# A running sum per block in a ring of buffers, and copies of it by ScalarE, in the message stage of a graph attention kernel

## The reference, cut to what matters

```python
# N = 2500 nodes, 80000 edges, F = 512 = 8 heads x 64
h_e = einsum('nf,hfd->hnd', layernorm(x), W_e)
alpha = leaky_relu(score of each edge and head)
ex = exp(alpha - m[src])
denom = segment_sum(ex, src)                      # per node and head
msg = ex[:, :, None] * h_e[dst]                   # per edge: a row of 512
out = segment_sum(msg, src) / (denom + EPS)       # per node
```

## Time and profile before

| | us |
|---|---|
| median of 3 runs | 3220.21 (3216.58 to 3222.29) |
| the profiled execution, its own time | 3229.66 |
| its span, from first to last instruction | 3227.9 |
| the message stage in it | about 1059, from 1833 to 2892 |

### The profile page before, as it was taken

One profiled execution on the slowest core, in us unless ns is written; L12 is line 12 of the kernel. 1 busy time (PEld: TensorE's weight loads), 2 busy tenths in 40 slices (PEclk: granted clock), 3 DMA queues, 4 the chain that ended last, 5 costly groups with the idle time before them and its releaser, 6 DMA issues. The chain is left out here.

```text
span 3227.9 us, 51758 instructions
## 1 busy us (share of the span) xinstructions
PE 2604.2 (81%) x16298; PEld 1661.5 (51%) x16298; DVE 2295.9 (71%) x4733; ACT 697.2 (22%) x1316; POOL 1545.2 (48%) x1568
## 2 busy tenths in 40 slices
PE   2499987799999999999990377878787777777898
PEld 2265653577777767776760244444444444446443
DVE  3577833699999989999999667667677676775222
ACT  1133320233333333333330100000000000004321
POOL 0223311466666666555650256556566565541244
PEclk9699998899999999999995588898888888889899
DMA  4022222877777777777773255555555555554443
GB/s 128 7 62 63 63 92 90 166 191 191 191 192 192 192 190 195 194 194 193 192 176 139 70 162 168 167 163 170 170 170 168 165 168 166 167 155 138 139 128 96
DMA packets 190342, 485.76 MB, mean 150 GB/s; under 512 B 47902, under 2 KB 77934, under 8 KB 189318
## 3 DMA queue, kind: packets, MB, share of 16 engines
q0 software_dynamic: 117200, 384.69, 44.2%
q1 hardware_dynamic: 48324, 71.73, 7.2%
q10 hardware_dynamic: 24562, 26.03, 2.8%
HBM read 437.29 MB, written 46.97 MB: 150 GB/s over the span
## 5 line engine op out<-in xcount | busy, mean ns | idle before, releaser
L1352 PE MATMUL ps_sum<-messages,node_onehot 128*125 128x512 f32 x1344 | 815.5, 701 | 238.8 <-DVE messages L1328 231.6
L1031 POOL DMA_INDIRECT rows_v<-target_rows,edge_dst x672 | 696.6, 1037 | 440.7 <-PE ps_heads L1126 234.9
L1307 POOL DMA_INDIRECT rows_e<-message_rows,edge_dst x672 | 635.2, 945 | 553.5 <-DVE messages L1328 219.8
L1080 DVE SCALAR_TENSOR_TENSOR z<-w_abs,corner 128x256 f32<-128x256 f32 x1344 | 559.8, 478 | 1.3 <-ACT w_abs L1144 1.3
L1099 PE MATMUL ps_u<-edge_space,source_onehot_t 125*128 x4032 | 515.5, 275 | 47.3 <-DVE source_onehot_t L1060 37.1
L1066 DVE TENSOR_TENSOR rows_v<-rows_v,ps_u 128x520 f32<-128x520 f32 x672 | 444.4, 690 | 91.3 <-PE ps_u L1099 51.0
L1144 ACT ACTIVATE w_abs<-ps_w 128x1024 f32<-128x1024 f32 x336 | 343.9, 1024 | 753.4 <-PE ps_w L1114 540.2
L1353 PEld LDWEIGHTS ps_den<-edge_space,node_onehot 128*125 128x125 f32 x1344 | 276.1, 205 | 373.9 <-issue 373.9
L1338 DVE TENSOR_TENSOR edge_space<-ps_sum,edge_space 125x512 f32 x336 | 231.2, 688 | 327.7 <-remote 201.9
L1099 PEld LDWEIGHTS ps_u<-edge_space,source_onehot_t 125*128 125x128 bf16 x4032 | 385.8, 97 | 119.3 <-issue 56.0
L1328 DVE TENSOR_TENSOR messages<-rows_e,ps_beside 128x1024 f32<-128x1024 f32 x336 | 406.8, 1211 | 6.6 <-DMA rows_e<-message_rows,edge_dst 6.3
(11 more groups left out here) (402 smaller groups left out, 2449.0 us busy)
## 6 DMA issues: line engine op xcount, KB each, us to landing
scores<-score SPq DMA_DIRECT2D x1344, 8.0 KB
edge_ids<-local_ids ACTq DMA_DIRECT2D x112, 187.5 KB
edge_space<-in_L_ffn_w_dram SPq DMA_DIRECT2D x24, 512.0 KB, 4.1
rows_v<-target_rows,edge_dst POOLq DMA_INDIRECT x672
rows_e<-message_rows,edge_dst POOLq DMA_INDIRECT x672
source_parts<-edge_space SPq DMA_DIRECT2D x20, 380.9 KB
edge_space<-source_parts SPq DMA_DIRECT2D x4, 1904.3 KB
edge_space<-scores SPq DMA_DIRECT2D x2, 2688.0 KB, 24.1
```

What stands on the lines that cost most here:

```text
L1031: nc.gpsimd.indirect_dma_start(rows[q][:, j, :], None, tab_v, bass.IndirectOffsetOnAxis(ap=edge["dst"][:, tile:tile + 1], axis=0)).then_in ...
L1080: ins = v.scalar_tensor_tensor(z[h][:, c, :], w_abs[h][:, c, :], corner[:, c:c + 1], w_abs[h][:, c, :], ALU.subtract, ALU.mult)
L1307: nc.gpsimd.indirect_dma_start(rows[q][:, j, :], None, tab_e, bass.IndirectOffsetOnAxis(ap=edge["dst"][:, tile:tile + 1], axis=0)).then_in ...
L1352: nc.tensor.matmul(ps_sum[h][:, :], onehot[h][:, j, :], messages[h][:, j, :], start=j == 0, stop=j == GROUP - 1)
```

## The change

- In the sorting stage DVE makes `same_block`: 1.0 where a group has the block of the group before it, else 0.0 (a memset of one column and one compare of 335).
- In the message stage PE writes both results of a group into one tile of two banks, `ps_both` (columns 0 to 511, and 512 to 519).
- `add_up(n)` on DVE is one instruction: running[n % 4] = running[(n - 1) % 4] * same_block[n] + ps_both. It has no register read. It waits for `e_summed`, for its own last one (`e_added`), and for ACT's copies of group n - 4 (`e_stored`).
- ACT, in `store(n)`, reads the block number into a register, waits for `e_added`, and copies the running sum to that block's place in `sums` and `denominators`, for every group. ACT's order is lay_weights(n), then store(n - 4).
- Four memsets of `running` stand ahead of the stage on DVE.

```diff
             def split_keys():
                 dve.wait_ge(keys_picked, 1)
                 v.tensor_copy(group_block[:, :], block_row[0:1, :])
+                v.memset(same_block[:, 0:1], 0.0)
+                v.tensor_tensor(same_block[:, 1:GROUPS], block_row[:, 1:GROUPS], block_row[:, 0:GROUPS - 1], ALU.is_equal)
...
-    BUFS, RING, TURN = 3, 6, 12
+    BUFS, RING, TURN, KEPT = 3, 6, 12, 4
...
-        ps_sum = [ctx.enter_context(nc.psum_tensor(f"ps_sum{h}", [L, F], F32)) for h in range(BUFS)]
-        ps_den = [ctx.enter_context(nc.psum_tensor(f"ps_den{h}", [L, 512], F32)) for h in range(BUFS)]
+        running = [sb(f"running{r}", [L, EW]) for r in range(KEPT)]
+        ps_both = [ctx.enter_context(nc.psum_tensor(f"ps_both{h}", [L, 1024], F32)) for h in range(BUFS)]
...
             def add_up(n, q, turn):
-
-                b = dve.value_load(group_block[0:1, DS(n, 1)], min_val=0, max_val=NB - 1)
                 at_least(dve, summed, n + 1)
                 at_least(dve, added, n)
-                total = sums[:, DS(b, 1), :].rearrange("p o f -> p (o f)")
-                v.tensor_tensor(total, ps_sum[q % BUFS][:, :], total, ALU.add)
-                den = denominators[:, DS(b, 1), :].rearrange("p o h -> p (o h)")
-                v.tensor_tensor(den, ps_den[q % BUFS][:, 0:HEADS], den, ALU.add).then_inc(added, 1)
+                at_least(dve, stored, 2 * (n - KEPT + 1))
+                v.scalar_tensor_tensor(running[n % KEPT][:, :], running[(n - 1) % KEPT][:, :], same_block[0:L, n:n + 1], ps_both[n % BUFS][:, 0:EW],
+                                       ALU.mult, ALU.add).then_inc(added, 1)
+
+            for r in range(KEPT):
+                ins = v.memset(running[r][:, :], 0.0)
+            link(ins)
             in_turns(TURNS, ((0, weigh), (2, add_up)), TURN)
...
-                    nc.tensor.matmul(ps_sum[h][:, :], onehot[h][:, j, :], messages[h][:, j, :], start=j == 0, stop=j == GROUP - 1)
-                    ins = nc.tensor.matmul(ps_den[h][:, 0:HEADS], onehot[h][:, j, :],
+                    nc.tensor.matmul(ps_both[h][:, 0:F], onehot[h][:, j, :], messages[h][:, j, :], start=j == 0, stop=j == GROUP - 1)
+                    ins = nc.tensor.matmul(ps_both[h][:, F:EW], onehot[h][:, j, :],
...
-            in_turns(TURNS, ((0, lay_weights),), TURN)
+            def store(n, q, turn):
+                b = act.value_load(group_block[0:1, DS(n, 1)], min_val=0, max_val=NB - 1)
+                at_least(act, added, n + 1)
+                at_least(act, stored, 2 * n)
+                nc.scalar.copy(sums[:, DS(b, 1), :].rearrange("p o f -> p (o f)"), running[n % KEPT][:, 0:F]).then_inc(stored, 1)
+                nc.scalar.copy(denominators[:, DS(b, 1), :].rearrange("p o h -> p (o h)"), running[n % KEPT][:, F:EW]).then_inc(stored, 1)
+
+            in_turns(TURNS, ((0, lay_weights), (4, store)), TURN)
```

More of the change, by code:

```diff
@@ L107, in _, with sort_and_project @@
             pool.sem_clear(range(first, last + 1))
-def sort_and_project(nc, a, const, edge, group_block, merged, x_sb, space, tab_v, tab_e, tab_parts, parts, parts_in, local_ids):
+def sort_and_project(nc, a, const, edge, group_block, same_block, merged, x_sb, space, tab_v, tab_e, tab_parts, parts, parts_in, local_ids):
     ident, ones, eps, row, rowb, identb, tri, col = (const[k] for k in ("ident", "ones", "eps", "row", "rowb", "identb", "tri", "col"))
@@ L1262, in _, with gather_messages @@
                 ins.then_inc(turned[b % 2], 1)
-def gather_messages(nc, const, edge, group_block, weights, tab_e, sums, denominators):
+def gather_messages(nc, const, edge, group_block, same_block, weights, tab_e, sums, denominators):
     row = const["row"]
-    BUFS, RING, TURN = 3, 6, 12
+    BUFS, RING, TURN, KEPT = 3, 6, 12, 4
     TURNS = GROUPS // TURN
@@ L1291, in gather_messages @@
         rows_laid, weights_laid = sem("node_rows_laid"), sem("weights_laid")
-        messages_set, summed, added = (sem(n) for n in ("messages_set", "e_summed", "e_added"))
+        messages_set, summed, added, stored = (sem(n) for n in ("messages_set", "e_summed", "e_added", "e_stored"))
         gathered = [sem(f"e_gathered{q}") for q in range(RING)]
@@ L1950, in program @@
         parts_in = sem("parts_in")
-        sort_and_project(nc, a, const, edge, group_block, merged, x_sb, edge_space[:, :], tab_v, tab_e, tab_parts, parts, parts_in, local_ids)
+        marks = ExitStack()
+        same_block = marks.enter_context(nc.sbuf_tensor("same_block", [P, GROUPS], F32))
+        sort_and_project(nc, a, const, edge, group_block, same_block, merged, x_sb, edge_space[:, :], tab_v, tab_e, tab_parts, parts, parts_in, local_ids)
         sums_space = edge_space[:, 0:NB * F]
@@ L1960, in program @@
             softmax_weights(nc, const, scores, keys, keys_in, carry, weights, sums_space[:, 0:PIECE], sums, denominators)
-        gather_messages(nc, const, edge, group_block, weights, tab_e, sums, denominators)
+        gather_messages(nc, const, edge, group_block, same_block, weights, tab_e, sums, denominators)
+        marks.close()
         ffn = {"up": sb("up_t", [P, KF, EXPERTS, 2 * INNER]), "down": sums_space[:, 0:EXPERTS * INNER // P * F].rearrange("p (e i f) -> p e i f", e=EXPERTS, f=F),
```

## The result

| | kernel before | changed kernel |
|---|---|---|
| median of 11 runs each, us | 3218.18 (3208.71 to 3225.06) | 3227.49 (3219.69 to 3232.12) |
| ratio | 1 | 1.0031, interval 1.0017 to 1.0045 |
| the profiled execution, us | 3229.66 | 3229.07 |

The changed kernel is slower by 9.3 us, outside the 0.2% that the prediction called no change, where 2.3 us less were forecast. The range of 3188 to 3275 us held the time. The two profiled executions don't show the loss, since that of before lay 11.5 us over the median of these 11 runs (9.45 us over that of the three runs known before); what a part costs has to be read from ratios over many runs.

A forecast was written before the change was run, and what follows sets the result against it. It took late counts of PE, with POOL's fetches and waits closing the sum, to bound the message stage; -3.5 + 0.8 + 0.4 = -2.3 us gave 3218 us from 3220.21, range 3188 to 3275.

The forecast's parts named there:

- Bound of the stage: Message stage: no engine full; PE's counts reach DVE late while gathers flow without a gap, and POOL's pause ends that.
- rival 1: Message stage: DVE's register read itself stands before the sum; 201.9 us would go, giving 3016; 7 in 100.
- POOL's pace closes the sum: Message stage: POOL's 837 us of fetches plus 219.8 us of waits for DVE make 1057 of 1059 us.
- DVE's sum: Message stage: one instruction of 0.753 us for two adds; taken 0, range 0 to -20 us, POOL's pace being slower.
- The register work: Message stage: block read leaves DVE's queue, saving 0.06 us at each of 59 stops: -3.5 us, at most -7.
- ACT's stores: Message stage: copies and reads, 270 us, fit into ACT's idle time and DVE's waits on them are covered: 0.
- The sum of -2.3 us: Whole kernel: -3.5 for register work, + 0.8 for ACT's last copies, + 0.4 in the sorting stage.
- PE, the memsets, the marks: Matmuls into one tile: 0; four memsets, at most 0.57 us each, hidden: 0; sorting stage's compare and memset: + 0.4 us.
- Rival 2: Message stage: stops shift; two fewer or more, 11 us, 3207 or 3229; 15 in 100 faster, 10 slower.
- Rival 3: Message stage: the new sum's scalar slows POOL's fetches through the shared port; 24 us, 3242, up to 3280; 10 in 100.
- Rival 4: Message stage: ACT's counts come late at DVE's wait for `stored`; 84 stops for 59, +93 us, 3311; 8 in 100.

The follow-up runs named there:

- `static_block_2`: Kernel before without DVE's register read, sums going to a constant block's place; late counts: 3209.98 us against 3211.31, ratio 0.9987.
- `in_place`: Kernel before with sums and denominators side by side, DVE adding each group by one instruction, register read kept; late counts: 3255.28 us against 3214.93, ratio 1.0120.
- `act_beside`: Kernel before plus ACT's register read, wait and two copies per group into a spare buffer, nobody waiting for them; prompt counts: 2961.98 us against 2961.19, ratio 1.0002.
- `act_beside_2`: Kernel before plus ACT's register read, wait and two copies per group into a spare buffer, nobody waiting; late counts: 3253.69 us against 3211.31, ratio 1.0109.
- `deep_4`: Kernel before with four buffers instead of three, sums added three groups behind, laid weights in SBUF instead of PSUM: 3146.92 us against 3173.17, ratio 0.9929.
- `read_beside`: Kernel before plus one register read and one wait for e_added per group on ACT, no copies; late counts: 3237.60 us against 3214.93, ratio 1.0071.

## Why the prediction was wrong

- **Bound of the stage.** Right that counts of PE come late and that DVE's register read has no part in it (rival 1 fell: "remote" 200.2 us without the read, `static_block_2` 0.9987). Wrong that they are late because gathers flow without a gap: with prompt counts the gathers flow at 210 GB/s without a stop, more than the 166 of before, and no count is over 0.02 us late. Wrong that POOL's pace closes the sum: it does so as arithmetic, but a ring of 12 showed that the 220 us are what DVE's waits leave over. With it falls the reason for taking DVE's sum at 0.
- **DVE's sum, 0 taken, 0 to -20.** Its time came out (0.751 for 0.753). The sum as a whole, without ACT, was worth -0.45%, -14 us, read and merging together: inside the bounds of the two terms (-27), not at the value taken. But one instruction in place of two is no gain as such, since `in_place` lost 1.2% with it.
- **The register work, -3.5.** 0.9987 with an interval that holds it and nothing as well. Not refuted, not shown.
- **ACT's stores, 0 taken.** This is the step that failed: that work on an idle engine adds nothing as long as DVE doesn't wait for it. The room was there (ACT busy 248.78 of 1059 us), no instruction waited for a store, and with it the kernel took 0.77% longer all the same (1.0032 against 0.9955), with DVE's waits for e_summed 13 us longer by one trace each. "Idle, so free" held where counts are prompt (`act_beside` 1.0002) and not where they are late (`act_beside_2` 1.0109). The sum of -2.3 us got its sign from leaving this out. Why it costs stays open. (Where the prediction says of an uncovered store that the third rival has its price, it is the fourth.)
- **PE, the memsets, the marks.** The memsets took 0.492 us each and hid; the marks, for which 0.4 us were taken, cost nothing that shows.
- **The rivals.** Rival 2 had 11 us for two stops fewer or more, a size like that found, but it named chance as its reason and the loss repeats: 1.0031, 1.0032, and 1.0039 without the marks. Rival 3 fell: a fetch takes 945 to 948 ns with the scalar and without it. So by the lock of which the prediction tells (the Trainium skill, "SBUF — State Buffer", section "SBUF: two separate sides") the scalar doesn't count as a second input in SBUF; `deep_4` shows what two do. Rival 4 named the right engine and the wrong way: 66 stops of 3.3 us and not 84, with no wait for `stored`.

The range held the time by its width, and the 3229 us of rival 2's slower case came near it by luck.

What stays open: why PE's counts are held at some times and not at others, whether that is a cost of tracing, and whether ACT's part lengthens the holding by an event of its own or only by shifting the work, as `in_place` did.

## What to carry to other kernels

Before tuning around a wait for which the profile names "remote", time the unchanged kernel again at another time: here the same program took 2961 and 3218 us, and where it took 2961 none of four edits of this stage showed. Work on an idle engine is not shown to be free while another engine waits for held counts; take its price from a run with the work laid beside, not from the room in its busy time, and expect that price to hold for this one arrangement alone. Where GpSimd's gathers set the pace, keep one operand of a long VectorE operation in PSUM; where held counts did, `deep_4` was the fastest kernel in spite of its slower fetches.

## What the runs showed of the hardware

- Counts of TensorE can be held and delivered in a batch, three within 0.19 us and up to 6.24 us after the modelled end (group 91 above), under one condition; under the other all 336 come within 0.02 us. The two conditions lie 257 us of 3218 apart, some 203 us of them in the message stage.
- The messages' multiplication (128x1024, 1.22 us) with both inputs in SBUF holds a gather issue of POOL that starts during it until 0.82 us after its end: 292 fetches of 1.49 us on average, beside 380 of 0.952. A fetch that was under way first is not held (275 cases).
- Less work on VectorE made the kernel slower (`in_place`: 22 us less work, 40 us more time), and so did a register read and a wait per group on an idle ScalarE (`read_beside`: 23 us). Both are measured under late counts alone.
